# Two sixteen-head attentions: the second half of the tokens normalised and turned between projections 1 and 2

## The chip, the cores and the metric

The kernel runs on one core of a Trainium2 chip. The metric is the device time of one execution in microseconds (us), smaller is better. The kernel before takes 867.09 us, the median of three runs (865.51 to 869.0).

The engines are named as in the profile: PE is TensorE, DVE VectorE, ACT ScalarE, POOL GpSimd, SP SyncE (it issues most of the DMAs).

## The reference

Two decoder layers on x of shape 4 x 256 x 256 (1024 tokens of 256 channels), in float32. Each has a self-attention, a cross-attention and a feed-forward part, and each part is x = x + f(layernorm(x)). The change is in the two self-attentions:

```
# layer 0: sixteen heads of 16 channels, with LoRA on every projection
q, k, v = (split(x @ W.T + b + 0.5 * (x @ Bm.T) @ Am.T) for each of q, k, v)
attn = softmax(einsum('bhqd,bhkd->bhqk', q, k) * 0.25)
out = einsum('bhqk,bhkd->bhqd', attn, v)      # then the o projection, likewise
...
# layer 1: sixteen heads of 16 channels, causal, with ALiBi slopes
qkv = x @ qkv_w.T + qkv_b
scores = where(causal, q @ k.T * 0.25 + slope * (key - query), -1e9)
out = softmax(scores) @ v @ out_w.T + out_b
```

Between and behind them stand a latent cross-attention, a quantised feed-forward part, a second cross-attention and a mixture of experts, which the change does not touch.

## The kernel before

The stages follow one another, each in a block of its own with one instruction stream per engine, written out by hand; semaphores tie the streams together, and every engine works through its stream in order. `attention_block` is called twice: for layer 0 (tiles a0_..., with `first`, which loads x and folds the LoRA products into the weights, and with `scales`, which reads the later weights on the side), and for layer 1 (`alibi=True`).

**The prologue.** The 1024 tokens are eight tiles of 128, in two halves of four. A half goes through these steps:

- `statistics(half)` and `inverse(half)` on DVE, with the square root in `root(half)` on ACT between them. The first half is normalised on DVE. For the second half DVE makes `offsets()` (minus mean times inverse deviation), and ACT normalises its tiles in `normalised(4)` to `normalised(7)` (L631).
- `turn(half)` on PE: eight transposes (L759) into banks 0 and 1 of the PSUM, which `turned(half)` on ACT copies to xnT (L625, two copies).
- `project(g)`, g from 0 to 7 (L774): two float32 matmuls of 128x512 (four records in the profile), even g for q and odd g for k, 0 to 3 for the first half of the tokens and 4 to 7 for the second, into bank 2 + g % 4. Project 4 waits for the second half's xnT.

Since the scores are made of bfloat16 products with float32 accuracy, each projection is split into three bfloat16 parts: `high(g)` on ACT (L645), `remainder(g)` on DVE (L504, what is left), `middle(g)` on ACT (L651) and the low part on POOL (L454). SP sends the parts to their rows in the tiles a_qs and a_ks, six DMAs for q and six for k in each of four groups (`send`, L381): group 0 holds projections 0 and 1, group 1 projections 2 and 3, and so on. ACT does its part of a projection in the order in which its stream has it, and so do DVE and SP.

**The items.** There are 16 items, of four heads and one batch entry each; items 0 to 3 use group 0, 4 to 7 group 1. Of each, PE makes the scores in four units (three in the causal stage), `scores(n, u)` (L811, or L819 and L824), in banks 0 and 1 in turn, and DVE takes the row maxima, `maximum(n, u)` (L522). POOL splits the maxima in two bfloat16 parts (L460, L463), PE turns them (`max_transpose`, L841), ACT copies them (`max_rows`, L656), and a DMA puts them as two more rows beside the parts. Then PE makes the scores again, turned and less their maxima (`scores_t`, L859 or L870), ACT takes the exponentials (L667) and PE the products with v (`product`, L889). The first two scores wait only for their rows:

```python
if u == 0 and n % 4 == 0:
    pe.wait_ge(part_in[n // 4].sem, part_in[n // 4].at(16 * 2 * TERMS))
if n > 0 or u > 1:
    pe.wait_ge(mx_done.sem, mx_done.at(UNITS * n + u - 1))
```

In the prologue the scores of items 0 to 2 are mixed with the last projections, with the output bias (`project_bias`, L795) and with the eight projections of v (`project_values`, L784), which go to the banks of projections 4 to 7 and so wait for `remainder(4)` to `remainder(7)`. After that a loop keeps the scores four items ahead of the products.

Of the kernel before, what the change touches and what calls it, by code (L numbers as in the profile page):

```python
# [273 lines left out]
def attention_block(c, st, name, wqk_in, wvo, bias_io, alibi=False, first=None, scales=None, last_loads=None, spare=None):  # L274
# [20 lines left out]
    with ExitStack() as tmp:  # L295
# [76 lines left out]
        with nc.Block() as block:  # L372
# [99 lines left out]
            def _(dve):  # L472
                def statistics(half):
                    if first is not None:
                        dve.wait_ge(first.x_in[half].sem, 16)
                    for t in range(half * HT, (half + 1) * HT):
                        dve.bn_stats(stats[:, t, :], c.x[:, t, :]).then_inc(stats_done.sem, 1)
                    for t in range(half * HT, (half + 1) * HT):
                        dve.wait_ge(stats_done.sem, stats_done.at(t + 1))
                        dve.bn_aggr(mv[:, t, :], stats[:, t, :]).then_inc(mv_done.sem, 1)  # L480
                    dve.wait_ge(mv_done.sem, mv_done.at((half + 1) * HT))
                    dve.tensor_scalar(std[:, some(half)], mv[:, some(half), 1], LN_EPS, None, ALU.add)\
                        .then_inc(var_done.sem, 1)

                def inverse(half):
                    dve.wait_ge(std_done.sem, std_done.at(half + 1))
                    dve.reciprocal(rstd[:, some(half)], std[:, some(half)]).then_inc(rstd_done.sem, 1)
                    dve.wait_ge(rstd_done.sem, rstd_done.at(half + 1))
# [6 lines left out]
                def offsets():  # L495
                    dve.scalar_tensor_tensor(nmr[:, :], mv[:, some(1), 0], -1.0, rstd[:, some(1)], ALU.mult, ALU.mult)\
                        .then_inc(rstd_done.sem, 1)

                def remainder(g):
                    w, ot, half = parts_of(g)  # L500
                    dve.wait_ge(hi_done.sem, hi_done.at(g + 1))
                    if g >= 2:
                        dve.wait_ge(lo_done.sem, lo_done.at(g - 1))
                    dve.scalar_tensor_tensor(rest[:, g % 2, :], c.ps[:, 2 + g % 4, :], bcol[:, w, ot:ot + 1],  # L504
                                             parts[:, w, ot, 0, half_cols(half)],
                                             ALU.add, ALU.subtract).then_inc(rest_done.sem, 1)
# [17 lines left out]
                def maxima(n):  # L524
                    for u in range(UNITS):
                        maximum(n, u)
# [27 lines left out]
                if first is not None:  # L554
                    for k in range(2):
                        dve.wait_ge(permuted.sem, permuted.at(4 * k + 4))
                        first.folded(dve, k, wqk[:, k, :, :])
                statistics(1)
                dve.wait_ge(bias_in.sem, bias_in.at(64))
                remainder(0)  # L560
                if first is not None:
                    first.cast_identity(dve)
                remainder(1)
                inverse(1)
                offsets()
                remainder(2)
                remainder(3)
                if first is not None:
# [1 line left out]
                    first.folded(dve, 3, wo)  # L570
                remainder(4)
                remainder(5)
                maxima(0)
                remainder(6)
                remainder(7)
                maxima(1)
                output_bias()
                maxima(2)
# [30 lines left out]
            def _(act):  # L609
# [32 lines left out]
                def high(g):  # L642
                    w, ot, half = parts_of(g)
                    act.wait_ge(proj.sem, proj.at(g + 1))
                    act.activation(parts[:, w, ot, 0, half_cols(half)], c.ps[:, 2 + g % 4, :],  # L645
                                   ACT.Identity, bias=bcol[:, w, ot:ot + 1]).then_inc(hi_done.sem, 1)
# [41 lines left out]
                turned(0)  # L688
                root(1)
                act.preload_act_table_set("natural_log_exp_and_others")  # L690
                high(0)
                high(1)
                middle(0)
                high(2)
                middle(1)
                normalised(4)
                high(3)
                middle(2)
                normalised(5)
                middle(3)  # L700
                normalised(6)
                normalised(7)
                turned(1)
                high(4)
                high(5)
                middle(4)
                high(6)
                middle(5)
                high(7)
                middle(6)  # L710
                middle(7)
                values(0)
                max_rows(0)
                values(1)
# [35 lines left out]
            def _(pe):  # L750
# [177 lines left out]
                if first is not None:  # L928
                    first.products(pe, 0)
                turn(0)  # L930
                for g in range(4):
                    project(g)
                if first is not None:
                    first.products(pe, 2)
                turn(1)
                project(4)
                project(5)
                scores(0, 0)
                scores(0, 1)
                project(6)  # L940
                scores(0, 2)
                project(7)
                scores(0, 3)
                project_bias()
                project_values(0)
                scores(1, 0)
                project_values(1)
# [1238 lines left out]
class ContextKeys:  # L2186
# [49 lines left out]
    def middle(self, act):  # L2236
        act.wait_ge(self.rest_done.sem, 1)
        act.activation(self.parts[:, 1, :], self.rest[:, :], ACT.Copy).then_inc(self.mid_done.sem, 1)
# [963 lines left out]
```

## Time and profile before

| | |
|---|---|
| median of three runs | 867.09 us (865.51 to 869.0) |
| the profiled execution | 868.19 us |
| its span in the trace | 866.4 us |
| mean granted clock of TensorE | 0.93 |
| busy: PE, PEld | 744.5 us (86%), 479.7 us (55%) |
| busy: DVE, ACT, POOL | 560.8 us (65%), 430.5 us (50%), 203.6 us (24%) |
| first attention, start of the first projection | 14.29 us |
| second attention, start of the first projection | 521.00 us |

The times in the timelines are us from the start of the span. PE is the matmuls, PEld the loads of their weights. The granted clock is a share of TensorE's full speed. A row of a timeline merges instructions of one kind that follow closely: start, length, engine, line, operation, written tile <- read tiles, shape, count; in brackets is the idle time of the engine before it and what ended that. Matmuls are pipelined, so a row's length has a tail that lies beside the next row.

### The profile page before, as it was taken

The numbers are of one execution on the slowest core, as the hardware profiler recorded it, in microseconds if no ns is written. First come the engines' busy times: TensorE is split into PE (matmuls) and PEld (weight loads), VectorE is DVE, ScalarE is ACT, GpSimd is POOL, SyncE is SP. The second block draws the span as 40 slices with busy tenths as digits, with TensorE's granted clock in tenths as the row PEclk, the third lists the DMA queues.
The fourth block names the chain that finished last, engine by engine and source line by source line (L and its number), as shares of the span: only waits on it lengthen the run. The fifth ranks groups of instructions, "written<-read, shape, count | busy, mean of one in ns | idle before, by whom it ended". The sixth has DMA issues, their size and how long they took to land. (4 is left out here: it accounts for less than half of the span.)

```text
span 866.4 us, 13304 instructions
## 1 busy us (share of the span) xinstructions
PE 744.5 (86%) x4826; PEld 479.7 (55%) x4826; DVE 560.8 (65%) x1081; ACT 430.5 (50%) x894; POOL 203.6 (24%) x300
## 2 busy tenths in 40 slices
PE   6999958998989999898876368999859999849998
PEld 3455646665666666665552253666533444438887
DVE  5568666655656565755648872566477999674866
ACT  4547732636354453636348755455255666623332
POOL 2413020113030303213043712231022111261440
PEclk9989998999999999999997786999957999958999
DMA  4615412201111120210014204130020233402111
GB/s 126 169 41 158 145 33 69 72 26 49 28 45 40 34 72 1 72 28 14 13 27 134 56 9 132 52 112 3 1 56 7 60 73 84 126 2 75 73 49 48
DMA packets 49759, 52.23 MB, mean 60 GB/s; under 512 B 10116, under 2 KB 40388, under 8 KB 49588
## 3 DMA queue, kind: packets, MB, share of 16 engines
q1 hardware_dynamic: 45718, 50.37, 21.0%
q10 hardware_dynamic: 3978, 1.02, 0.5%
q8 instruction: 39, 0.64, 0.3%
q14 instruction: 24, 0.20, 0.1%
HBM read 26.58 MB, written 2.04 MB: 33 GB/s over the span
## 5 line engine op out<-in xcount | busy, mean ns | idle before, releaser
L522 DVE TENSOR_REDUCE a_nm<-ps 128x2 f32<-128x512 f32 (+1 forms) x112 | 75.5, 689 | 33.1 <-PE ps L824 19.8
L2512 DVE TENSOR_REDUCE x_nm<-ps 128x2 f32<-128x512 f32 x128 | 85.0, 687 | 12.7 <-PE ps L2653 10.5
L2597 ACT ACTIVATE x_pt<-ps 128x1024 f32<-128x1024 f32 x64 | 62.5, 1021 | 35.0 <-PE ps L2681 34.3
L1446 ACT ACTIVATE m_junk<-ps,m_nm 128x256 bf16<-128x256 f32 x128 | 58.6, 484 | 36.7 <-DVE m_nm L1309 36.7
L1283 DVE TENSOR_TENSOR m_qcs<-ps,mw_tab 128x512 f32<-128x512 f32 x96 | 61.8, 686 | 22.1 <-PE ps L1569 21.2
L1569 PE MATMUL ps<-m_xp,m_mp 128*128 128x512 f32 x288 | 74.4, 399 | 1.6 <-DVE m_wr L1297 1.6
L1269 POOL TENSOR_SCALAR fw<-fw,finv 128x256 f32<-128x256 f32 x24 | 11.6, 481 | 255.5 <-PE ps L1649 255.5
L2653 PE MATMUL ps<-kx,a_qs 96*128 96x256 bf16 x256 | 53.3, 297 | 8.2 <-DMA a_qs<-a_ks 6.5
L1569 PEld LDWEIGHTS ps<-m_xp,m_mp 128*128 128x128 f32 x288 | 51.9, 190 | 13.7 <-issue 4.5
L3028 PE MATMUL ps<-x_xp,x_wp 128*128 128x512 f32 x216 | 54.9, 405 | 0.0
L3028 PEld LDWEIGHTS ps<-x_xp,x_wp 128*128 128x128 f32 x216 | 40.7, 194 | 8.7
L2697 PE MATMUL ps<-x_pt,a_ks 128*32 128x256 f32 x512 | 41.8, 399 | 2.6 <-DVE x_av L2521 2.6
L2653 PEld LDWEIGHTS ps<-kx,a_qs 96*128 96x128 bf16 x256 | 20.8, 102 | 41.7 <-issue 13.6
L1309 DVE TENSOR_REDUCE m_nm<-ps 128x2 f32<-128x512 f32 x64 | 40.0, 683 | 3.4 <-PE ps L1608 3.2
L1332 DVE TENSOR_TENSOR m_cp<-ps,m_cp 128x256 fp32r<-128x256 f32 x32 | 12.8, 422 | 43.8 <-ACT m_cp L1472 43.8
L2681 PE MATMUL ps<-a_qs,kx 98*128 98x512 bf16 x128 | 39.9, 395 | 0.0
L1608 PE MATMUL ps<-m_kHH,m_qs 128*128 128x256 f32 x128 | 35.9, 318 | 4.3 <-DVE m_qs L1302 4.2
L1648 PE MATMUL ps<-m_qs,m_kHH 128*128 128x512 f32 x64 | 27.7, 433 | 12.9 <-issue 8.8
L667 ACT ACTIVATE a_pt<-ps 128x1024 f32<-128x1024 f32 x32 | 32.1, 1020 | 12.2 <-PE ps L859 12.2
L1466 ACT ACTIVATE m_pt<-ps 128x1024 f32<-128x1024 f32 x32 | 31.1, 1018 | 13.4 <-PE ps L1649 13.4
L667 ACT ACTIVATE fw<-ps 128x1024 f32<-128x1024 f32 (+1 forms) x32 | 25.8, 810 | 22.0 <-PE ps L875 21.9
L1339 DVE TENSOR_TENSOR x<-ps,x 128x512 f32<-128x512 f32 x32 | 22.1, 692 | 21.7 <-PE ps L1679 19.6
(302 smaller groups left out, 1726.2 us busy)
## 6 DMA issues: line engine op xcount, KB each, us to landing
a_qs<-a_parts SPq DMA_DIRECT2D x48, 128.0 KB
a_ks<-a_parts SPq DMA_DIRECT2D x48, 128.0 KB
m_q<-m_qs SPq DMA_DIRECT2D x32, 128.0 KB
x_gb<-scr_g SPq DMA_DIRECT2D x8, 512.0 KB, 3.8
fw<-in_f_w SPq DMA_DIRECT2D x12, 256.0 KB
a_qs<-a_ks SPq DMA_DIRECT2D x48, 64.0 KB
mw_wq<-in_m_wq SPq DMA_DIRECT2D x8, 256.0 KB, 2.8
mw_wo<-in_m_wo SPq DMA_DIRECT2D x8, 256.0 KB, 2.9
```

What stands on the lines that cost most here:

```text
L522: dve.tensor_reduce(dst, src, AX.X, ALU.max, negate=True).then_inc(mx_done.sem, 1)
L667: act.activation(pt[:, n % 2, kt, 0:banks * BANK], c.ps[:, 2 + 2 * kt:2 + 2 * kt + banks, :].rearrange("p b n -> p (b n)"), ACT.Exp, scale ...
L1283: dve.tensor_tensor(qcs[:, half, tile, cs, :].rearrange("p (b q) -> p b q", q=SEQ), c.ps[:, QB_BANKS[k], :].rearrange("p (b q) -> p b q", ...
L1309: dve.tensor_reduce(nm[:, k // 4, first:first + QT], c.ps[:, S_BANKS[k % 4], :].rearrange("p (t k) -> p t k", t=QT), AX.X, ALU.max, negate ...
L1446: act.activation(junk[:, n % 4, :], c.ps[:, S_BANKS[k % 4], qt * SEQ:(qt + 1) * SEQ], ACT.Exp, bias=nm[:, k // 4, one], accum_out=den[:, k ...
L1569: mm = pe.matmul(c.ps[:, QB_BANKS[k], :], mp[:, p % 2, w, dt, tile * P:(tile + 1) * P], xp[:, x, dt, half_cols(half)], start=((dt, w, x) = ...
L2512: dve.tensor_reduce(nm[:, n % ITEMS, QT * u:QT * u + QT], c.ps[:, u % 2, :].rearrange("p (t k) -> p t k", t=QT), AX.X, ALU.max, negate=Tru ...
L2597: act.activation(pt[:, n % 2, kt, :], c.ps[:, 2 + 2 * kt:4 + 2 * kt, :].rearrange("p b n -> p (b n)"), ACT.Exp, scale=SCALE).then_inc(exp_ ...
L2653: mm = pe.matmul(c.ps[:, u % 2, qt * SEQ:(qt + 1) * SEQ], queries(slice(0, S_ROWS), n, u).squeeze(1)[:, qt * P:(qt + 1) * P], kx[0:S_ROWS, ...
L2681: mm = pe.matmul(c.ps[:, 2 + 2 * kt + h // 2, :], kx[0:T_ROWS, g, b * SEQ + kt * P:b * SEQ + (kt + 1) * P], queries(slice(0, T_ROWS), n, h ...
L2697: mm = pe.matmul(c.ps[rows(h), 6, 0:SEQ], vs[:, QT * b + kt, g, :], pt[:, n % 2, kt, h * SEQ:(h + 1) * SEQ], start=(kt == 0), stop=(kt == ...
L3028: mm = pe.matmul(up_bank(j, half), wp[:, b, w, at:at + EH], xp[:, x, dt, cols(half)], start=((dt, w, x) == terms[0]), stop=((dt, w, x) == ...
```

## The change

The order of the work in the prologue, in both attentions. What is computed stays the same, and no instruction is added or removed.

- DVE: `inverse(1)` and `offsets()` come right behind `statistics(1)`, ahead of `remainder(0)`. Further down, `remainder(6)` and `remainder(7)` stand behind the first and the second maximum of item 0; they stood behind all of its maxima.
- ACT: the four normalisations of the second half come ahead of `high(0)`; they stood one by one between the parts of projections 1 to 3. `turned(1)` comes behind `middle(0)`. The parts of the other projections follow in one rule, `high(g)` and then `middle(g - 1)`.
- PE: `turn(1)` comes behind `project(1)`; it stood behind the LoRA products that follow `project(3)`. The scores of item 0 come one place later each: unit 0 before `project(6)`, unit 1 before `project(7)`, unit 2 before the output bias and unit 3 behind it.

```diff
--- before.py
+++ after.py
@@ -556,13 +556,13 @@
                         dve.wait_ge(permuted.sem, permuted.at(4 * k + 4))
                         first.folded(dve, k, wqk[:, k, :, :])
                 statistics(1)
+                inverse(1)
+                offsets()
                 dve.wait_ge(bias_in.sem, bias_in.at(64))
                 remainder(0)
                 if first is not None:
                     first.cast_identity(dve)
                 remainder(1)
-                inverse(1)
-                offsets()
                 remainder(2)
                 remainder(3)
                 if first is not None:
@@ -570,9 +570,12 @@
                     first.folded(dve, 3, wo)
                 remainder(4)
                 remainder(5)
-                maxima(0)
+                maximum(0, 0)
                 remainder(6)
+                maximum(0, 1)
                 remainder(7)
+                for u in range(2, UNITS):
+                    maximum(0, u)
                 maxima(1)
                 output_bias()
                 maxima(2)
@@ -688,27 +691,18 @@
                 turned(0)
                 root(1)
                 act.preload_act_table_set("natural_log_exp_and_others")
+                for t in range(HT, TT):
+                    normalised(t)
                 high(0)
                 high(1)
                 middle(0)
+                turned(1)
+                middle(1)
                 high(2)
-                middle(1)
-                normalised(4)
-                high(3)
-                middle(2)
-                normalised(5)
-                middle(3)
-                normalised(6)
-                normalised(7)
-                turned(1)
-                high(4)
-                high(5)
-                middle(4)
-                high(6)
-                middle(5)
-                high(7)
-                middle(6)
-                middle(7)
+                for g in range(3, NG):
+                    high(g)
+                    middle(g - 1)
+                middle(NG - 1)
                 values(0)
                 max_rows(0)
                 values(1)
@@ -928,20 +922,22 @@
                 if first is not None:
                     first.products(pe, 0)
                 turn(0)
-                for g in range(4):
-                    project(g)
+                project(0)
+                project(1)
+                turn(1)
+                project(2)
+                project(3)
                 if first is not None:
                     first.products(pe, 2)
-                turn(1)
                 project(4)
                 project(5)
                 scores(0, 0)
+                project(6)
                 scores(0, 1)
-                project(6)
+                project(7)
                 scores(0, 2)
-                project(7)
+                project_bias()
                 scores(0, 3)
-                project_bias()
                 project_values(0)
                 scores(1, 0)
                 project_values(1)
```

TensorE, first attention, from the first half's transposes (L759 before, L753 now) on; L774 and L768 are the projections, L162 the LoRA products, L811 and L805 the scores. Before:

```order
L759 MATMUL ps<-ident,xn 128x128 x8
L774 MATMUL ps<-xnT,a_wqk 128x512 x8
L162 MATMUL ps<-a_pt 128x256 x4
L759 MATMUL ps<-ident,xn 128x128 x8
L774 MATMUL ps<-xnT,a_wqk 128x512 x4
L811 MATMUL ps<-a_ks,a_qs 128x256 x4
L774 MATMUL ps<-xnT,a_wqk 128x512 x2
L811 MATMUL ps<-a_ks,a_qs 128x256 x2
L774 MATMUL ps<-xnT,a_wqk 128x512 x2
L811 MATMUL ps<-a_ks,a_qs 128x256 x2
```

And now:

```order
L753 MATMUL ps<-ident,xn 128x128 x8
L768 MATMUL ps<-xnT,a_wqk 128x512 x4
L753 MATMUL ps<-ident,xn 128x128 x8
L768 MATMUL ps<-xnT,a_wqk 128x512 x4
L162 MATMUL ps<-a_pt 128x256 x4
L768 MATMUL ps<-xnT,a_wqk 128x512 x4
L805 MATMUL ps<-a_ks,a_qs 128x256 x2
L768 MATMUL ps<-xnT,a_wqk 128x512 x2
L805 MATMUL ps<-a_ks,a_qs 128x256 x2
L768 MATMUL ps<-xnT,a_wqk 128x512 x2
L805 MATMUL ps<-a_ks,a_qs 128x256 x2
```

The second eight transposes stand between the projections 1 and 2, and every pair of score matmuls has two projection matmuls ahead of the next one.

ScalarE, first attention, from the second table load on: L645 (now L648) are the high parts, L651 (L654) the middle parts, L631 (L634) the normalised tiles, L625 (L628) the copies of the turned half. Before:

```order
L690 ACT_TABLE_LOAD
L645 ACTIVATE a_parts<-ps,a_bcol 128x512 x2
L651 ACTIVATE a_parts<-a_rest 128x512
L645 ACTIVATE a_parts<-ps,a_bcol 128x512
L651 ACTIVATE a_parts<-a_rest 128x512
L631 ACTIVATE xn<-x,a_nmr,a_rstd 128x256
L645 ACTIVATE a_parts<-ps,a_bcol 128x512
L651 ACTIVATE a_parts<-a_rest 128x512
L631 ACTIVATE xn<-x,a_nmr,a_rstd 128x256
L651 ACTIVATE a_parts<-a_rest 128x512
L631 ACTIVATE xn<-x,a_nmr,a_rstd 128x256 x2
L625 ACTIVATE xnT<-ps 128x512 x2
```

And now:

```order
L693 ACT_TABLE_LOAD
L634 ACTIVATE xn<-x,a_nmr,a_rstd 128x256 x4
L648 ACTIVATE a_parts<-ps,a_bcol 128x512 x2
L654 ACTIVATE a_parts<-a_rest 128x512
L628 ACTIVATE xnT<-ps 128x512 x2
L654 ACTIVATE a_parts<-a_rest 128x512
L648 ACTIVATE a_parts<-ps,a_bcol 128x512 x2
L654 ACTIVATE a_parts<-a_rest 128x512
L648 ACTIVATE a_parts<-ps,a_bcol 128x512
L654 ACTIVATE a_parts<-a_rest 128x512
```

The four normalisations stand directly behind the table load, and the copies of the turned half between the first and the second middle part.

## Rows read from the trace of the kernel before

**Rows 1.** Timeline of TensorE, first attention: start us, us, engine line op, [idle before]
```profile
14.29 9.01 PE L774 MATMUL ps<-xnT,a_wqk 128*128 128x512 f32 x16 [0.69 <-ACT xnT L625]
23.23 1.99 PE L162 MATMUL ps<-a_pt 16*128 16x256 f32 x8
25.15 0.45 PE L759 MATMUL ps<-ident,xn 128*128 128x128 f32 x2
26.12 0.33 PE L759 MATMUL ps<-ident,xn 128*128 128x128 f32 x1 [0.52 <-ACT xn L631]
...
28.11 5.40 PE L774 MATMUL ps<-xnT,a_wqk 128*128 128x512 f32 x8 [0.74 <-ACT xnT L625]
33.35 0.60 PE L811 MATMUL ps<-a_ks,a_qs 96*128 96x256 bf16 x4
```

**Rows 2.** Stretches of 2 us: busy time of each engine, PEclk, DMA share, GB/s
```profile
28.00:30.00 2.00, 1.89 (x3) 0.85 (x4) 0.00 (x0) 0.06 (x1) 0.00 (x0) 0.58 0.74 201
38.00:40.00 2.00, 2.00 (x12) 1.67 (x11) 1.96 (x4) 1.08 (x2) 0.14 (x1) 1.00 0.61 165
40.00:42.00 2.00, 2.00 (x13) 1.58 (x12) 1.61 (x4) 1.34 (x4) 1.86 (x2) 1.00 0.01 4
56.00:58.00 2.00, 2.00 (x17) 0.55 (x13) 0.69 (x1) 0.37 (x1) 0.00 (x0) 0.50 0.00 0
538.00:540.00 2.00, 2.00 (x4) 0.84 (x3) 0.00 (x0) 0.00 (x0) 0.00 (x0) 0.50 0.70 200
```

**Rows 3.** Timeline of ScalarE, first attention
```profile
14.56 1.28 ACT L690 ACT_TABLE_LOAD   x1
18.11 0.69 ACT L645 ACTIVATE a_parts<-ps,a_bcol 128x512 bf16<-128x512 f32 x1 [2.27 <-PE ps L774]
...
22.73 0.59 ACT L631 ACTIVATE xn<-x,a_nmr,a_rstd 128x256 f32<-128x256 f32 x1
```

**Rows 4.** Timeline of TensorE, second attention
```profile
521.00 9.94 PE L774 MATMUL ps<-xnT,fw 128*128 128x512 f32 x16 [0.69 <-ACT xnT L625]
...
532.72 0.33 PE L759 MATMUL ps<-ident,xn 128*128 128x128 f32 x1 [1.32 <-ACT xn L631]
533.76 1.82 PE L759 MATMUL ps<-ident,xn 128*128 128x128 f32 x6 [0.71 <-ACT xn L631]
536.26 5.71 PE L774 MATMUL ps<-xnT,fw 128*128 128x512 f32 x8 [0.69 <-ACT xnT L625]
541.81 0.39 PE L819 MATMUL ps<-a_ks,a_qs 102*128 102x128 bf16 x4
```

**Rows 5.** Timeline of TensorE, first attention, later
```profile
42.99 0.27 PE L841 MATMUL ps<-identb,a_nms 128*8 128x128 bf16 x2 [0.65 <-POOL a_nms L463]
...
49.86 1.03 PE L859 MATMUL ps<-a_qs,a_ks 98*128 98x256 bf16 x8 [0.80 <-issue]
...
53.34 0.61 PE L811 MATMUL ps<-a_ks,a_qs 96*128 96x256 bf16 x2
...
59.12 0.38 PE L811 MATMUL ps<-a_ks,a_qs 96*128 96x256 bf16 x2
...
62.32 0.38 PE L811 MATMUL ps<-a_ks,a_qs 96*128 96x256 bf16 x2
...
98.08 0.60 PE L903 MATMUL ps<-ident,xn 128*128 128x128 f32 x4
```

**Rows 6.** Timeline of VectorE, first attention
```profile
21.50 0.86 DVE L496 SCALAR_TENSOR_TENSOR a_nmr<-a_mv,a_rstd 128x4 f32<-128x4 f32 x1
```

**Rows 7.** Timeline of SyncE's DMA issues, first attention
```profile
25.97 0.60 SPq L381 DMA_DIRECT2D a_ks<-a_parts  x1
...
36.31 1.90 SPq L381 DMA_DIRECT2D a_ks<-a_parts  x3
```

**Rows 8.** Timeline of ScalarE, second attention
```profile
524.82 0.69 ACT L645 ACTIVATE a_parts<-ps,a_bcol 128x512 bf16<-128x512 f32 x1 [2.48 <-PE ps L774]
```

**Rows 9.** Timeline of SyncE's DMA issues, second attention
```profile
533.35 0.60 SPq L381 DMA_DIRECT2D a_ks<-a_parts  x1
```

## The prediction

> **What bounds the kernel now.** I read the two prologues in the timelines engine by engine, because the shares of busy time and the chain that ended last (it reaches back only to the last stage) say nothing of them. In both, the work between the first projection and the first item's scores hangs on TensorE: it runs projections 0 to 3 without a gap [rows 1, 4], then stops in the middle of turning the second half, for xn tiles that ScalarE has not written and for the copies of the turned half (the waits on L631 and L625) [rows 1, 4]. ScalarE makes those tiles one by one between its copies of the projections: the first one starts at 22.73 us [rows 3]. Nothing forced it to be so late: ScalarE sat idle for 2.27 us after its table load, and for 2.48 us in the second attention, until projection 0 was done [rows 3, 8].
>
> The gaps are followed by slow projections. TensorE's granted clock was 0.58 of full speed from 28 us on and 0.50 around 539 us (that is the 1.2 GHz level, against 2.4) after the gapped transposes [rows 2], and projections 4 and 5 took 5.24 us (28.11 to 33.35) and 5.55 us (536.26 to 541.81) [rows 1, 4].
>
> **What a projection costs at full speed.** Projection 0 ran slow, until 18.05 us (ScalarE's copy starts at 18.11) [rows 3]; the next three ended when the LoRA products start at 23.23 [rows 1]: 5.18 / 3 = 1.73 us each. Four transposes take 0.60 us at full speed (the last row) [rows 5]; eight are at most 1.2 us, and laid close together some 1.05.
>
> **The change, part by part.**
>
> *VectorE: inverse and offsets ahead of remainder 0.* Nothing is added, two small operations of 0.2 and 0.86 us [rows 6] move into a stretch in which VectorE waits for ScalarE's first copy. They are due after root(1), which ends before the table load at 14.56, so the offsets are there by about 15.7. Cost 0.
>
> *ScalarE: four normalisations ahead of high(0).* One takes 0.59 us [rows 3], four in a row some 2.1. The table load ends at 15.84, so they end at 17.95, while high(0) could not start before 18.11. In the second attention the idle 2.48 us before 524.82 [rows 8] hold them too. The cover is TensorE's slow projection 0; were it gone, SyncE's first issue would slip by up to 2.1 us. Cost 0, bounds 0 to 0.5.
>
> *TensorE: turn(1) after projection 1.* It starts at about 19.8 and 527.5 with its tiles ready. turned(1) on ScalarE (two copies, about 0.6 us each) is due only for projection 4, behind two projections. Before, turning cost 25.15 to 28.11 = 2.96 us; now 1.05: **1.91 saved** [rows 1]. In the second attention projection 3 ends at 521.00 + 9.94 less a tail of 0.15 = 530.8, and projection 4 starts at 536.26 [rows 4]: 5.46 less 1.05 = **4.41 saved**.
>
> *Clock.* Without the gaps I expect TensorE to keep full speed from projection 1 on, so projections 4 and 5 cost 3.46 us: 5.24 - 3.46 = **1.78** and 5.55 - 3.46 = **2.09** saved. Bounds: 0 each if the clock drops all the same.
>
> *ScalarE's later order.* turned(1) stands ahead of middle(1), and middle(3) now behind high(4). SyncE is the one who waits for them, and its queue has its own pace: the last of group 0's twelve issues starts at 25.97, and the queue is full until 36.31 + 1.90 [rows 7]. middle(1) still starts near 22.2, and middle(3), at about 28.7, is due only when the queue comes to it after 30. remainder(5), which needs GpSimd's low part 3 (one operation after middle(3)), is free by about 30.5, when its own high part is. Cost 0.
>
> *TensorE: scores(0, u) one place later each, and VectorE's remainders 6 and 7 between the maxima.* No work is added. By my walk through the waits, the bank of every score is free ahead of its turn, by 0.1 us for scores(1, 0), which waits for the maximum behind remainder 7, and by more for the others. What goes is a wait of 0.65 us on GpSimd before the first max_transpose [rows 5]: GpSimd was still making low parts, and these now come earlier against TensorE's order. **0.65 saved**, bounds 0 and 0.65. The second attention shows no such wait.
>
> *Are the rows there?* Scores(0, 0) needs the twelve DMAs of group 0. The last of the queue's three issues in 1.90 us [rows 7] begins at about 37.6, and the data stopped within 38 to 40 us (share 0.61 against 0.74 when full, then 0.01) [rows 2], at about 39.65: 2.05 us from issue to landing. So group 0 lands at 28.0 in the first attention, where TensorE now comes at 33.35 - 3.69 = 29.66: no wait. In the second the last issue starts at 533.35 [rows 9] and lands at 535.4, and TensorE would come at 541.81 - 6.50 = 535.3: it waits a little. I take **0.2 back**, bounds 0 and 1.5.
>
> After that both stages run in the same order as before. From scores(0, 0) to the loop TensorE is the engine that others wait for, and the loop's items follow one another at 3.20 us (59.12 to 62.32) [rows 5], so a start that is earlier by so much ends the stage earlier by as much; the loads that follow are issued by queues that wait for the items, and move along.
>
> **Sum.** First attention 1.91 + 1.78 + 0.65 = 4.34. Second 4.41 + 2.09 - 0.2 = 6.3. Together 10.6 of the profiled execution's 868.19 us: 857.6. The median of the three runs is 1.1 lower than that execution; I take half of this off, since part of its excess may be clock that I have counted already: **857.0 us**.
>
> **Rivals.**
> 1. *A second slow stretch goes as well.* In the first attention the clock was 0.50 again around 57 us [rows 2], and the loop's first item took 5.78 us (53.34 to 59.12) against 3.20 [rows 5]. Before it TensorE had waited 0.80 us at 49.86 and more behind. With all starting 4.3 us earlier, this sparse piece may no longer bring the clock down: 2.6 us more, 855.0. For it: the piece is only just sparse. Against: its own wait (values, then the first transposed scores) is untouched. 0.15.
> 2. *The DMA rows become the wait.* If a group takes 3.5 us to land instead of 2.05, the second attention waits 1.5 us, and the first still none: 858.9 from the sum, less the same half, 858.4. For it: the second attention has no margin at all. Against: SyncE's pace is the same as before. 0.10.
> 3. *One slow stretch stays in each attention*, at another place, for instance behind the transposes or at the values. That gives the clock terms back: 1.78 + 2.09, 860.9. 0.10.
> 4. *Slower.* The transposes themselves bring the clock down. In both attentions the fall came at or behind them, at 28 us and in the six that took 1.82 us at 533.76 [rows 2, 4]; they now stand in the middle of the projections. If TensorE then ran at half speed from turn(1) to projection 5, projections 2 and 3 (3.46), the products (23.23 to 25.15, 1.92) and 4 and 5 (3.46) would each cost double in the first attention, 8.8 us, and 6.9 in the second: 857.0 + 15.7 = 872.7. It decides from the point where more than 10.6 us of such work is slowed. Against it: later in the stage transposes of the same form stand between other work, and run at full speed (0.60 for four) [rows 5]. 0.03. The Trainium skill speaks for this rival: its page "TensorE: Matmul & The Clock Gate", section "Part 4: PE-mode transpose", says that transposes in this mode do not bring the full clock about. By that rule 1 us of them in each attention counts like the gap it replaces, and the time would be somewhere from 857 up to the 872.7; the trace does not tell the rule from the gaps, which are both there.
>
> **How the numbers follow.** The forecast has 0.62, the rivals 0.15, 0.10, 0.10 and 0.03. A measurement of this kernel tells a difference from none at about 0.5%, 4.3 us, that is below 862.8. The forecast and rivals 1 and 2 are all faster, and most of rival 3 too, of which I give 0.06 to no difference, for a case in which more than one stretch moves in elsewhere. So faster 0.91, same 0.06, slower 0.03. The range goes from rival 1, with 2 us for the spread of the runs and of the clock further down the program, 853.0, to just over rival 3, 861.5.
>
> **What would show it.** Right: in the changed profile turn(1) stands at about 19.8 and 527.5 - 4.3 without a gap, PEclk is 1.00 from there through projection 5, the first scores start near 29.7 and, in the second attention, 14.3 us after projection 0 starts instead of 20.8. No wait on GpSimd stands before the first max_transpose. Wrong, step by step: an idle before projection 4 (turned(1) too late), an idle before the first scores that a DMA ends (rival 2), PEclk of 0.5 in projections 2 to 5 (rivals 3 and 4), or a stage that starts its loop early and yet ends as late as before. Each would be read against the start of scores(0, 0), which is the one number that carries most of the sum.

## The result and the profile after

The changed kernel takes 854.33 us, the median of four runs (852.75 to 854.85), against 867.89 us for four runs of the kernel before (865.51 to 869.0). The ratio is 0.9849, 95% interval 0.9808 to 0.989: faster by 1.5%. The forecast was 857.0 us within 853.0 to 861.5; faster was right, and the time is 2.7 us below the forecast, near rival 1. The profiled execution took 854.85 us with a span of 853.0 us, 13.4 less than before.

Of its page, the line of the granted clock in 40 slices of 21.3 us (9 is 90% or more of full speed; the third slice, 43 to 64 us, was an 8 before):

```profile
PEclk9999989999999999999997788999858999969999
```

TensorE, first attention, the rows that answer to [rows 1, 5] (start us, us, engine, line, operation; in brackets the idle time before):

```profile
14.28 6.30 PE L768 MATMUL ps<-xnT,a_wqk 128*128 128x512 f32 x8 [0.69 <-ACT xnT L628]
20.42 1.04 PE L753 MATMUL ps<-ident,xn 128*128 128x128 f32 x8
21.30 3.60 PE L768 MATMUL ps<-xnT,a_wqk 128*128 128x512 f32 x8
24.82 1.99 PE L162 MATMUL ps<-a_pt 16*128 16x256 f32 x8
26.74 3.70 PE L768 MATMUL ps<-xnT,a_wqk 128*128 128x512 f32 x8
30.28 0.39 PE L805 MATMUL ps<-a_ks,a_qs 96*128 96x256 bf16 x2
...
39.20 0.27 PE L835 MATMUL ps<-identb,a_nms 128*8 128x128 bf16 x2
...
46.07 1.03 PE L853 MATMUL ps<-a_qs,a_ks 98*128 98x256 bf16 x8 [0.80 <-issue]
...
49.40 0.38 PE L805 MATMUL ps<-a_ks,a_qs 96*128 96x256 bf16 x2
...
52.59 0.38 PE L805 MATMUL ps<-a_ks,a_qs 96*128 96x256 bf16 x2
```

The gap is gone. The eight transposes at 20.42 take 0.88 us until the next row, and of the rows shown behind the one at 14.28, none before 46.07 has an idle time. The first scores start at 30.28, 16.0 us after projection 0; before, it was 33.35 - 14.29 = 19.06. No wait for GpSimd stands before the first max_transpose (39.20). The loop's first item takes 52.59 - 49.40 = 3.19 us, where it had been 5.78 [rows 5].

ScalarE, first attention, the rows that answer to [rows 3]:

```profile
14.54 1.28 ACT L693 ACT_TABLE_LOAD   x1
15.84 2.07 ACT L634 ACTIVATE xn<-x,a_nmr,a_rstd 128x256 f32<-128x256 f32 x4
18.10 0.69 ACT L648 ACTIVATE a_parts<-ps,a_bcol 128x512 bf16<-128x512 f32 x1 [0.19 <-PE ps L768]
...
21.73 1.07 ACT L628 ACTIVATE xnT<-ps 128x512 f32<-128x512 f32 x2
```

The four normalisations take 2.07 us and leave 0.19 us before projection 0 is done. The cover held, with little to spare. The copies of the turned half stand at 21.73, long before projections 4 and 5 want them at 26.74, where TensorE waits for nothing.

TensorE, second attention, answering to [rows 4]:

```profile
509.28 2.30 PE L753 MATMUL ps<-ident,xn 128*128 128x128 f32 x8 [5.55 <-DVE xn L492]
512.26 6.48 PE L768 MATMUL ps<-xnT,fw 128*128 128x512 f32 x8 [0.69 <-ACT xnT L628]
518.58 1.04 PE L753 MATMUL ps<-ident,xn 128*128 128x128 f32 x8
519.46 7.03 PE L768 MATMUL ps<-xnT,fw 128*128 128x512 f32 x16
527.10 0.40 PE L813 MATMUL ps<-a_ks,a_qs 102*128 102x128 bf16 x4 [0.61 <-DMA a_ks<-a_parts]
```

Projections 2 to 5 are one row of 7.03 us. From projection 0 to the first scores it is 14.84 us instead of 20.81. The first scores now wait 0.61 us for a DMA. SyncE's issues there, answering to [rows 9]:

```profile
524.59 0.61 SPq L381 DMA_DIRECT2D a_ks<-a_parts  x1
```

The last issue of group 0 starts at 524.59 and its data are taken at 527.10: 2.5 us.

The clock, in stretches of 2 us (length; busy PE, PEld, DVE, ACT, POOL; PEclk; DMA share; GB/s), answering to [rows 2]: behind the first attention's second turning, at the loop's first item, and behind the second attention's turning. It is full in all three.

```profile
20.00:22.00 2.00, 2.00 (x12) 1.39 (x11) 0.66 (x1) 1.38 (x3) 0.10 (x1) 1.00 0.72 190
50.00:52.00 2.00, 2.00 (x25) 0.83 (x24) 1.71 (x3) 1.28 (x2) 0.33 (x2) 1.00 0.02 6
518.00:520.00 2.00, 2.00 (x12) 1.32 (x11) 0.50 (x1) 1.22 (x3) 0.00 (x0) 1.00 0.69 197
```

**Where the 13.4 us are**, from the starts of the same work in both traces:

| stretch | before | after | less |
|---|---|---|---|
| first attention: projection 0 to the loop's second item | 14.29 to 59.12 | 14.28 to 52.59 | 6.5 |
| from there to the second attention's projection 0 | to 521.00 | to 512.26 | 2.2 |
| second attention: to its first scores | to 541.81 | to 527.10 | 6.0 |
| from there to the last stage's first long row | to 775.81 | to 760.82 | 0.3 |
| last stage, to the end of the span | to 866.4 | to 853.0 | -1.6 |

The second, fourth and fifth lines lie where the change moves nothing. Most of the 2.2 us of the second are the clock's. The same four matmuls behind the first attention, in the kernel before, in the changed kernel and in the repeated profile of the changed kernel (the last experiment below):

```profile
146.08 2.74 PE L1583 MATMUL ps<-m_qcs,m_wr 128*128 128x512 f32 x4
138.22 1.88 PE L1579 MATMUL ps<-m_qcs,m_wr 128*128 128x512 f32 x4
138.46 2.70 PE L1579 MATMUL ps<-m_qcs,m_wr 128*128 128x512 f32 x4
```

The granted clock was 0.55 from 146 to 148 us in the first, 1.00 from 138 to 140 in the second and 0.50 there in the third, which runs the same kernel as the second. From the transposes ahead of these matmuls to the row behind them it is 148.26 - 143.13 = 5.13 us, 139.54 - 136.05 = 3.49 and 140.59 - 135.46 = 5.13. So 1.6 of the 2.2 us are a slow stretch that the changed kernel has in one execution and not in the other: no gain of the change, but luck of the profiled pair.

The last stage gave 1.6 us back. There, a wait stands that the kernel before did not show:

```profile
784.23 3.04 PE L3024 MATMUL ps<-x_xp,x_wp 128*128 128x512 f32 x12
788.88 1.70 PE L3036 MATMUL ps<-x_wp,x_hTp 128*128 128x256 f32 x12 [1.61 <-DVE x_hTp L2958]
```

Its chain of waits leads to the DMA of the gate values, x_gb<-scr_g, 4.10 us. The same wait (1.64 us) stands in the repeated profile of the changed kernel, and not in that of the first experiment below, whose span is 850.8 us with nearly the same order. It is in both profiles of the changed kernel and in two of the others below (`project(6)` first, 1.58 us, and both small edits, 1.56), so whether it belongs to this kernel or comes and goes with the run is not shown. That the 2.2 us ahead and the 1.6 us here nearly cancel is luck.

### The profile page after: what moved, and what is told of

The parts are those of the page before. It is cut to its first block and busy times, and to the rows that moved or that the text cites. A ratio compares the mean times of both kernels' runs of the same rounds, so it can differ in the third digit from the quotient of the medians.

```text
span 853.0 us, 13304 instructions
## 1 busy us (share of the span) xinstructions
PE 733.0 (86%) x4826; PEld 474.5 (56%) x4826; DVE 557.7 (65%) x1081; ACT 429.7 (50%) x894; POOL 203.1 (24%) x300
```

## The experiments

My theory (A): the gain is the gap in turning the second half, together with the slow clock behind it. Rivals: (B) the new order of scores and remainders carries a good part; (C) part of the gain is luck of the clock elsewhere; (D) the transposes bring the clock down. The kernel before, run beside each group of kernels, had medians of 866.86, 865.49, 868.89 and 867.25 us over 11 to 20 runs each, and single runs from 859.4 to 874.2. Differences between groups are therefore read by their ratios.

### The turning alone

The changed kernel with these pieces in the old order:

```diff
                 scores(0, 0)
-                project(6)
                 scores(0, 1)
-                project(7)
+                project(6)
                 scores(0, 2)
-                project_bias()
+                project(7)
                 scores(0, 3)
+                project_bias()
...
-                maximum(0, 0)
-                remainder(6)
-                maximum(0, 1)
-                remainder(7)
-                for u in range(2, UNITS):
-                    maximum(0, u)
+                maxima(0)
+                remainder(6)
+                remainder(7)
```

> The changed kernel, but with item 0's scores and VectorE's remainders 6 and 7 in the order of before. Theory A (the gain is the gap in turning the second half and the slow projections behind it): all but the 0.65 us wait on GpSimd in the first attention is kept, so 854.5 to 856 us, and that wait is back before the first max_transpose. Rival B (the order of scores and remainders carries a good part, since it lets VectorE start the maxima and GpSimd finish the low parts earlier): 859 to 863 us.

853.89 us (852.6 to 855.36, six runs), ratio 0.9841 (0.9807 to 0.9876): the whole gain, with the median 0.6 us below the range that I gave. In its trace the wait for GpSimd is back, at the place of [rows 5]:

```profile
39.99 0.27 PE L832 MATMUL ps<-identb,a_nms 128*8 128x128 bf16 x2 [0.64 <-POOL a_nms L463]
```

Rival B falls. The 0.65 us term is real in the trace, and is not seen in the time, which carries more noise than that.

### The order of the scores alone

The opposite: the kernel before with only those pieces in the new order.

> The kernel before, but with item 0's scores and VectorE's remainders 6 and 7 in the new order. Theory A: the 0.65 us wait alone goes, 866.5 to 868 us (before 867.9). Rival B: 860 to 864 us.

866.44 us (862.52 to 869.46, twelve runs), ratio 0.9988 (0.9959 to 1.0017): no change that can be told.

### One attention at a time

`attention_block` twice in the program, once as before and once as changed, each attention calling its own.

> The whole change in the first attention alone, the second as before. By the two traces the first attention's last matmuls and the next stage start 6.3 us earlier: 861.0 to 862.0 us if nothing is gained or lost behind it. Rival C (a part of the gain is luck of TensorE's clock in stages that the change does not touch, which shift against each other): more than 1.5 us away from that.

> The whole change in the second attention alone. By the traces, from its first projection to its first scores it takes 14.84 us instead of 20.81, 6.0 less: 861.4 to 862.4 us. Rival C: more than 1.5 us away from it, with the sum of the gains of this and the run before unlike the 13.6 us of both together.

The first alone: 860.89 us (858.74 to 863.06), ratio 0.9919 (0.9893 to 0.9945). The second alone: 859.05 us (852.98 to 861.71), ratio 0.9895 (0.9851 to 0.9938). The ratios multiply to 0.9815, within the interval of both together (0.9808 to 0.989), so the gains add within the noise. Against that group's 866.86 the first took 6.0 us off, where 6.3 were expected. The second took 7.8 us off, 1.8 more than its own stretch's 6.0. Its median lies 2.3 us below its range, more than the 1.5 that I had set for rival C; the sum of the two gains, 13.8 us, is not unlike the 13.6 of both together. Its runs spread over 8.7 us. Its profile shows one place where such a spread can come from. Its first attention is the untouched one, with the same gap. TensorE and its clock there:

```profile
26.96 0.33 PE L759 MATMUL ps<-ident,xn 128*128 128x128 f32 x1 [0.53 <-ACT xn L631]
...
28.95 3.70 PE L774 MATMUL ps<-xnT,a_wqk 128*128 128x512 f32 x8 [0.74 <-ACT xnT L625]
```

```profile
28.00:30.00 2.00, 1.26 (x5) 0.57 (x4) 0.00 (x0) 0.90 (x2) 0.00 (x0) 1.00 0.74 202
52.00:54.00 2.00, 1.91 (x22) 1.14 (x22) 2.00 (x4) 1.03 (x2) 0.40 (x2) 1.00 0.01 2
```

The clock did not fall behind the gap, and projections 4 and 5 took 3.70 us instead of 5.40. Nor did it fall at 52 us, where the kernel before had this, and stayed at 0.50 until 58 us [rows 2]:

```profile
52.00:54.00 2.00, 1.79 (x10) 0.70 (x10) 1.74 (x4) 0.80 (x2) 0.09 (x1) 0.56 0.00 0
```

In the profile of the scores experiment, with the same gap, it was at 0.50 in both places. The same instructions with the same idle times thus run at either level, from one execution to the next. That is the first attention; in the second, with its longer gap, the clock was at 0.50 behind the gap in all three profiles that have the old order there (the kernel before, the scores experiment and the first-only one). Rival C is right to this extent: by these profiles the gap does not cost its clock part in each run, it risks it, and 1.6 us of the profiled pair's difference are the clock in a stretch that the change does not touch.

### Turning late, with the tiles early

The changed kernel with `turn(1)` behind `project(3)` (and the products) again, and the copies behind the middle part 3:

```diff
                 project(1)
-                turn(1)
                 project(2)
                 project(3)
                 if first is not None:
                     first.products(pe, 2)
+                turn(1)
                 project(4)
...
                 middle(0)
-                turned(1)
                 middle(1)
                 high(2)
-                for g in range(3, NG):
+                high(3)
+                middle(2)
+                middle(3)
+                turned(1)
+                high(4)
+                for g in range(5, NG):
                     high(g)
                     middle(g - 1)
```

> The changed kernel, but with the second half turned where it was before, behind projection 3 (its tiles are written early, as in the change, and its copies follow the middle part 3). TensorE then waits only for the two copies, 0.7 us in each attention, not for the tiles. Theory A (long gaps bring the clock down, and the transposes only stand beside them): the clock holds, projections 4 and 5 take 3.5 us together, and the time is 0.7 us up for each attention, 855 to 857 us. Rival D (transposes ahead of a short wait bring the clock down as before): projections 4 and 5 take over 5 us and the time is 858 us or more.

856.17 us (854.7 to 861.5, eight runs), ratio 0.9909 (0.9878 to 0.994). TensorE in the second attention:

```profile
522.42 1.04 PE L757 MATMUL ps<-ident,xn 128*128 128x128 f32 x8
525.78 3.70 PE L772 MATMUL ps<-xnT,fw 128*128 128x512 f32 x8 [2.32 <-ACT xnT L628]
```

In the first attention the wait is 0.74 us, as expected. In the second my edit cost more: 2.32 us, since ScalarE had its middle part 3 to make first. Even so the clock held in both attentions of this profile, and the two projections took 3.70 us. In this profile the clock held over a single gap of 2.32 us right behind eight transposes; rival D's 5 us did not appear. Early tiles alone thus bring most of the gain (0.9% of 1.5% by the ratios, whose intervals overlap); the place of `turn(1)` covers the copies' wait.

### Forty transposes instead of eight

In the changed kernel, the second half's eight transposes are made four times more ahead of the real ones:

```diff
+                    for again in range(4 if half else 0):
+                        for dt in range(DT):
+                            for j in range(HT):
+                                t = half * HT + j
+                                if dt == 0 and again == 0:
+                                    pe.wait_ge(xn_done.sem, xn_done.at(t + 1))
+                                pe.transpose(c.ps[:, dt, j * P:(j + 1) * P], c.xn[:, t, dt * P:(dt + 1) * P],
+                                             c.ident[:, :])
                     for dt in range(DT):
                         for j in range(HT):
```

> The changed kernel, with the eight transposes of the second half made five times (the same output), so that 40 transposes stand between projections 1 and 2. If transposes keep TensorE's clock up like other matmuls, they add 32 x 0.11 = 3.5 us in each attention, less the 0.6 us wait for the DMA rows in the second: 860.5 to 861.5 us, and PEclk stays at 1.00 behind them. If they count as idle (rival 4 of the prediction, and the page's rule), projections 2 to 5 behind them run at half speed for a stretch in each attention: 864 us or more, and PEclk of 0.5 there.

861.13 us (858.47 to 863.4, twelve runs), ratio 0.9941 (0.9908 to 0.9973), in the middle of the first range. TensorE's row of the extra transposes in the first attention, the real ones, and the clock through and behind them:

```profile
19.97 3.66 PE L754 MATMUL ps<-ident,xn 128*128 128x128 f32 x32
23.46 1.04 PE L761 MATMUL ps<-ident,xn 128*128 128x128 f32 x8
24.33 3.60 PE L776 MATMUL ps<-xnT,a_wqk 128*128 128x512 f32 x8
```

```profile
22.00:24.00 2.00, 2.00 (x20) 2.00 (x19) 0.00 (x0) 0.00 (x0) 0.62 (x1) 1.00 0.73 193
24.00:26.00 2.00, 2.00 (x9) 1.10 (x8) 0.00 (x0) 1.60 (x3) 0.22 (x1) 1.00 0.50 135
526.00:528.00 2.00, 2.00 (x21) 2.00 (x20) 0.50 (x1) 0.23 (x1) 1.16 (x1) 1.00 0.53 149
```

4.4 us of nothing but transposes, and PEclk stays at 1.00, in them and in the projections behind. The third stretch lies in the second attention's 40, where it is the same. Rival 4 of the prediction does not hold here. The Trainium skill's page "TensorE: Matmul & The Clock Gate", section "Part 4: PE-mode transpose", says that the full clock does not engage in transposes and that they don't count as busy in the same way. As far as keeping the clock goes this trace does not agree (1.00 through 40 of them), and the measurement decides. Whether transposes alone bring a fallen clock up was not tested.

### The gap filled, nothing moved

The kernel before, with transposes of the identity in the gaps between the tiles (three each in the first attention, six in the second, and six behind the last there):

```diff
+                def filler(count, bank, j):
+                    for k in range(count):
+                        pe.transpose(c.ps[:, bank, j * P:(j + 1) * P], c.ident[:, :], c.ident[:, :])
...
                             if dt == 0:
+                                if half and j:
+                                    filler(6 if alibi else 3, 0, j)
                                 pe.wait_ge(xn_done.sem, xn_done.at(t + 1))
...
                         mm.then_inc(xn_tr.sem, 1)
+                    if half and alibi:
+                        filler(6, 7, 0)
```

> The kernel before, with nothing moved, but with extra transposes of the identity (into a bank that is overwritten or unused) in the gaps in which TensorE waits for the tiles of the second half: 9 in the first attention, 24 in the second. The waits stay. If the slow projections 4 and 5 come from the gaps, the clock holds in both attentions, projections 4 and 5 take 3.7 us instead of 5.4 and 5.7, and the time falls by the clock's part alone, less up to 1.5 us for the extra work: 862 to 865 us. If the clock falls all the same, it is 867 us or more.

858.89 us (858.21 to 860.46, six runs), ratio 0.9898 (0.9857 to 0.994), below the range that I gave. TensorE in the second attention, and the clock there and in the first:

```profile
527.80 0.71 PE L765 MATMUL ps<-ident,xn 128*128 128x128 f32 x5
528.35 0.82 PE L753 MATMUL ps<-ident 128*128 128x128 f32 x6
529.25 3.70 PE L782 MATMUL ps<-xnT,fw 128*128 128x512 f32 x8
```

```profile
28.00:30.00 2.00, 1.94 (x5) 0.98 (x6) 0.00 (x0) 0.01 (x1) 0.00 (x0) 1.00 0.74 201
52.00:54.00 2.00, 2.00 (x26) 0.83 (x24) 1.71 (x3) 1.28 (x2) 0.36 (x2) 1.00 0.02 6
528.00:530.00 2.00, 1.92 (x13) 1.42 (x12) 0.00 (x0) 1.09 (x2) 0.00 (x0) 1.00 0.72 202
```

The tiles come as late as before: from projection 0 to projection 4 it is 529.25 - 514.16 = 15.09 us, where it was 15.26 [rows 4]. What is different is the clock: it holds at 28, at 52 and at 529 us. From projection 0 to the first scores it is 532.79 - 514.16 = 18.63 us, 2.2 less than before, 2.0 of it in projections 4 and 5 (3.54 us instead of 5.55); the change takes it to 14.84 by also removing the wait. This is the cleanest separation I have: beside the change's 1.5%, a kernel that keeps its gap and fills it gains 1.0% (0.6 to 1.4% by its interval). The time of the gap itself fits the rest: the first scores come 1.5 us (17.52 against 16.00) and 3.8 us later after projection 0 than in the changed kernel. Also, these six runs lie within 2.3 us of each other, where the kernel before spreads over 10.

### Two small edits and a third

What was left in the changed kernel's prologue: 0.61 us before the first scores in the second attention, and 0.80, 0.57 and 0.21 us around the first transposed scores. The first edit puts `project(6)` ahead of `scores(0, 0)` in the second attention, the second mixes item 3's scores with the first transposed ones. Shown is the second:

```diff
-                scores_t(0, 0)
-                scores_t(0, 1)
-                all_scores(3)
+                scores(3, 0)
+                scores(3, 1)
+                scores_t(0, 0)
+                scores(3, 2)
+                scores_t(0, 1)
+                scores(3, 3)
                 max_transpose(2)
```

> The changed kernel, with projection 6 ahead of the first scores in the second attention, where the changed kernel waits 0.61 us for the rows' DMAs. Theory: the wait is filled, 0.4 to 0.6 us off, 853.5 to 854 us, within what can be told from no change. Rival: the first maximum starts later and a score waits for its bank instead, no gain.

> The changed kernel, with item 3's first two scores ahead of the first transposed scores and its other two between and behind them, in both attentions. There TensorE waits 0.8 us for ScalarE's last copy of the values, and later 0.6 and 0.2 us for VectorE's maxima. Theory: the scores fill the first wait, VectorE's maxima start earlier and the other two waits go, 1.0 to 1.5 us off in each attention, 851.5 to 852.5 us. Rival E: the stage is bound elsewhere from there on (VectorE's 3.2 us an item in the first, TensorE in the second), and at most 0.5 us each comes off, 853.3 us or more.

> The changed kernel with both small edits together (projection 6 ahead of the first scores in the second attention, and item 3's scores around the first transposed scores in both). The two touch different waits: alone they took about 1 and 3.5 us off. If they add, 849 to 850.5 us; if the second attention's start is bound by VectorE's maxima once both are in, no better than the second edit alone, 850.8 us.

The first edit: 853.33 us (851.48 to 855.35), ratio 0.9867 (0.983 to 0.9903), not to be told from the changed kernel; the wait is gone from its trace (projections 2 to 6 are one row). The second: 850.81 us (849.22 to 855.86), ratio 0.9844 (0.9804 to 0.9884). Its median lies 3.5 to 4.7 us under the changed kernel's 854.33 and 855.53, but those were measured beside other runs of the kernel before, and by the ratios (0.9849 and 0.986) no gain can be told. Both together: 850.99 us (845.98 to 853.94), ratio 0.9784 (0.9738 to 0.9829). They don't add in the medians, and with these spreads I can't say more. TensorE with the second edit, first attention:

```profile
44.62 0.60 PE L805 MATMUL ps<-a_ks,a_qs 96*128 96x256 bf16 x4
45.58 0.60 PE L853 MATMUL ps<-a_qs,a_ks 98*128 98x256 bf16 x4 [0.35 <-issue]
46.01 0.38 PE L805 MATMUL ps<-a_ks,a_qs 96*128 96x256 bf16 x2
...
50.46 0.38 PE L805 MATMUL ps<-a_ks,a_qs 96*128 96x256 bf16 x2
```

Of the three waits 0.35 us is left. The loop's second item starts 50.46 - 14.21 = 36.25 us after projection 0, 2.1 us sooner than in the changed kernel (38.31).

The third edit adds 20 transposes of the identity at the start of the second attention to the kernel with both:

```diff
+                if alibi:
+                    for k in range(20):
+                        pe.transpose(c.ps[:, 7, (k % 4) * P:(k % 4 + 1) * P], c.ident[:, :], c.ident[:, :])
                 turn(0)
```

> The kernel with both small edits, and 20 extra transposes of the identity at the start of the second attention, where TensorE waits 5.5 us for the first normalised tiles and then makes its transposes and projection 0 and a part of projection 1 at half speed. If activity alone decides the clock, it is up again before or in projection 0, and 1.5 to 2.5 us come off: 847.5 to 849 us. If the work before does not matter, nothing comes off, 849.8 us.

849.71 us (848.75 to 851.14, six runs), ratio 0.979 (0.9749 to 0.9831), against 0.9784 without it on the same chip: nothing. Its trace shows why:

```profile
504.39 2.38 PE L926 MATMUL ps<-ident 128*128 128x128 f32 x20 [1.05 <-PEq L1894]
508.84 1.74 PE L753 MATMUL ps<-ident,xn 128*128 128x128 f32 x8 [2.07 <-DVE xn L492]
511.51 6.71 PE L768 MATMUL ps<-xnT,fw 128*128 128x512 f32 x8 [0.94 <-ACT xnT L628]
```

The twenty ran at full speed at once and took 2.38 us, which fills less than half of the 5.55 us wait, so 2.07 us were left idle before the real transposes, and projections 0 and 1 still took 6.71 us. The attempt did not test what it was meant to: how the clock would be after a start with no idle time stays open.

### The changed kernel once more

> The changed kernel itself, unaltered, in as many rounds as the experiments had, since the kernel before has run between 859.4 and 874.2 us by now, by chip and by run. If the first four runs (852.8 to 854.9) were typical, 853 to 855.5 us and a ratio of 0.983 to 0.987 to the kernel before. If they fell together by luck, the spread is wider than 4 us, as with the kernel before, and the median above 856 us.

855.53 us (853.31 to 856.29, six runs), ratio 0.986 (0.9824 to 0.9896). All ten runs of the changed kernel lie within 3.5 us, while the eleven of the kernel before beside these six go from 862.7 to 871.1.

## Why the prediction was right, and where it was off

- **The covers** (VectorE's offsets, ScalarE's four normalisations, the copies, SyncE's queue): right. The closest was the table load and the normalisations ahead of high(0), due at 17.95 and ended at 17.91, 0.19 us ahead.
- **The gap, 1.91 and 4.41 us**: right. The transposes take 0.88 us against the 1.05 taken.
- **The clock behind it, 1.78 and 2.09 us**: right for the profiled pair. In the first attention projections 4 and 5 take 3.54 us instead of 5.24 (3.46 was taken), and in the second, projections 2 to 5 are one row of 7.03 us, at the same pace. But as a term it was of another kind than I wrote: in the first attention the same gap left the clock up in one profile of the untouched order and brought it down in two. It is a part of the median, and of the spread.
- **Projections 0 and 1** were taken as 5.5 us in the first attention. They took 6.14 in the profiled execution (14.28 to 20.42) and 5.0 in the repeated one. The clock rises at another moment in each run, and no term stood for it. That put 0.6 us on the wrong side here.
- **0.65 us of GpSimd**: gone as said, and too small to be told in the kernel's time.
- **"I take 0.2 back"**, the rows' DMAs in the second attention: mis-sized. The wait was 0.61 us, since issue to landing is 2.5 us there and not the 2.05 that I had read from the end of the data. The bound of 1.5 held it, and filling the wait (the first small edit) gained nothing that could be told. Rival 2, with 3.5 us to land, did not come.
- **Rival 1, with 0.15**, is what the profile shows: the loop's first item takes 3.19 us. This is 2.6 us that the sum left out, the main part of the 2.7 us by which the forecast was high. (As a gain the miss is 3.5 us: 10.1 were forecast from the three runs' 867.09, and 13.6 measured from the four runs' 867.89.) The step that failed is that I argued from the sparse stretch at 49 us, which the change leaves as it is, and gave the fall at 52 us its own chance. It is tied to the first one: of the profiles with the old order, both in which the clock fell at 28 us had it fall again at 51 to 52, and both in which it held at 28 held it there too, and in no profile of the changed order did either happen. Why the two go together I did not test.
- **Rivals 3 and 4** needed a clock that falls behind the transposes. It did not, not even behind forty.
- **Outside the two attentions** 2.2, 0.3 and -1.6 us moved, 0.9 in sum, with nothing changed there. No term stood for them, and that they nearly cancel is luck. So is the half of the 1.1 us that was taken off for the profiled execution: no run tests it.

## What to carry to other kernels

Look where the engine that bounds a stage waits for work that another engine could have done while idle: here four 0.6 us operations stood 7 us later in ScalarE's stream than need be, and moving them needed no faster instruction. Here a wait on TensorE could cost more than its length, when the clock fell with it for the projections behind it; price both, and price the clock as a risk, by several runs rather than by one trace. Where a gap can't be closed, a few transposes in it are cheap: here they gave 1.0% where the change gives 1.5%, with nothing moved.

## What the runs showed that I had not expected

- The clock's fall is not fixed by the instruction stream. With the same gap, projections 4 and 5 are a row of 5.40 us in one profile and of 3.70 in another. The kernel before ran from 859.4 to 874.2 us, and the spread goes with the clock: of its 61 runs beside the experiments, the 19 with a mean granted clock of 0.929 or less took 868.9 to 874.2 us, and the 7 with 0.940 or more 859.4 to 863.9. The kernel with the gap filled and the changed kernel kept within 2.3 and 3.5 us.
- VectorE's offsets of the second half (L496, 128x4) took 0.87 us each in the kernel before and 0.16 us in the changed one, where they run earlier. In the kernel before, both ran beside a GpSimd operation (the low part, L454) and ended with it, within 0.02 us: at 22.36 and 22.35, and at 530.00 and 529.99. In the changed kernel GpSimd was idle at either place. No run moves GpSimd's operation alone, so the cause is not shown; they are on no path here.
- Transposes hold the full clock: 4.4 us of them at PEclk 1.00.
- Filling the gap took about 9 us off by the ratio (10.0 between the two profiles), where the two slow pairs of projections come to 3.7 and the slow item at 52 us to 2.6. Of the rest, 2.3 us lie between the loop's second item and the second attention, and 1.6 of them are the slow stretch at 144 to 148 us of the kernel before, which the filled one lacks (3.48 us from 137.68 to 141.16, at 1.00). Since the changed kernel has that stretch in one profile of two, I take this part for luck of the run rather than the filling's; that was not tested.
